# One long run of projections per unit on TensorE, and turns of B in the gate banks

## The reference

```python
proj = einsum('bsd,ed->bse', layernorm(x), in_proj_w)      # gate 8192, x 8192, B 1024, C 1024, dt 128
hBC = silu(causal_conv4(x, B, C))                          # depthwise, 4 taps, plus bias
xch = hs * dt                                              # 128 heads of 64, 4 chunks of 128 tokens
Y_diag = einsum('bzlhn,bzshn,bhzls,bzshp->bzlhp', C, B, L, xch)   # inside a chunk
states = einsum('bzlhn,bhzl,bzlhp->bzhpn', B, decay_states, xch)  # per chunk, then carried on
Y_off = einsum('bzlhn,bzhpn,bhzl->bzlhp', C, prev_states, exp(A_cum))
y = (Y_diag + Y_off + hs * D) * silu(gate)
out = rmsnorm over each of 8 groups of 1024 (y) * norm_w @ out_proj_w.T
```

## Time and profile before

| | |
|---|---|
| median of 3 runs | 1702.21 us (1701.96 to 1703.28) |
| profiled execution | 1699.52 us, span 1697.8 us |
| TensorE busy | 1624.3 us, 96% |
| VectorE busy | 1361.0 us, 80% |
| ScalarE busy | 1140.6 us, 67% |
| GpSimd busy | 836.5 us, 49% |
| mean granted TensorE clock | 0.986 of full |

### The profile page before, as it was taken

How to read it: one execution, slowest core, us unless ns; L and a number is a source line. 1 busy time by engine, 2 the same in 40 slices (tenths; PEclk the granted TensorE clock), 3 DMA queues, 4 the chain that set the end, 5 groups by cost and what they waited for, 6 DMA issues and landing times.

```text
span 1697.8 us, 26883 instructions
## 1 busy us (share of the span) xinstructions
PE 1624.3 (96%) x9616; PEld 1348.5 (79%) x9616; DVE 1361.0 (80%) x1974; ACT 1140.6 (67%) x2002; POOL 836.5 (49%) x543
## 2 busy tenths in 40 slices
PE   7779999999999999999999999999999999999987
PEld 5668888888888888878888888888888788888876
DVE  6467787987789878897879878898788978798766
ACT  5477767776687667767677766866677676777721
POOL 1135544564455544465445644555444654456542
PEclk9789999999999999999999999999999999999989
DMA  5423232323323232322323232222323223232211
GB/s 199 174 91 110 81 107 86 108 71 116 96 86 100 91 104 87 110 93 80 108 85 109 70 115 97 91 94 95 102 84 110 95 80 107 87 107 80 84 41 50
DMA packets 88244, 164.56 MB, mean 97 GB/s; under 512 B 23344, under 2 KB 39728, under 8 KB 87856
## 3 DMA queue, kind: packets, MB, share of 16 engines
q1 hardware_dynamic: 88112, 162.85, 29.2%
HBM read 157.03 MB, written 5.77 MB: 96 GB/s over the span
## 4 chain that ended last, share of the span: by engine, by line
PE 65%; DVE 13%; issue 9%; POOL 6%; ACT 3%; DVEq 0%; POOLq 0%; ACTq 0%
PE g_bank L713 6%; PE g_bank L715 6%; PE g_bank L714 6%; PE x_bank L713 5%; PE x_bank L715 4%; PE x_bank L714 4%; PE state_bank L722 4%; PE d_bank L731 4%; DVE mixed L1173 4%; PE state_bank L738 4%; PE x_bank L772 3%; PE x_bank L770 3%; PE x_bank L771 3%; PE d_bank L772 3%; PE d_bank L770 3%
## 5 line engine op out<-in xcount | busy, mean ns | idle before, releaser
L1323 POOL TENSOR_TENSOR y<-y,gate 128x512 f32<-128x512 f32 x128 | 223.3, 1744 | 457.5 <-DVE y L1140 457.5
L930 ACT ACTIVATE scores<-scores,tables 128x128 f32<-128x128 f32 x1024 | 312.4, 390 | 1.7 <-DMA scores<-sums_dram 1.7
L1078 DVE SCALAR_TENSOR_TENSOR hs<-x_bank,cols,hs 128x1022 f32<-128x1022 f32 (+2 forms) x192 | 244.7, 1274 | 85.2 <-ACT hs L940 82.9
L713 PE MATMUL g_bank<-x_high,w_high 128*128 128x512 f32 x624 | 258.8, 415 | 0.7 <-DVE bc L1156 0.7
L1330 POOL TENSOR_TENSOR xdecay<-xdt,tables 128x384 f32<-128x384 f32 x128 | 144.2, 1127 | 227.6 <-DVE xdt L1150 227.6
L715 PE MATMUL g_bank<-x_high,w_low 128*128 128x512 f32 x624 | 246.5, 395 | 0.0
L714 PE MATMUL g_bank<-x_low,w_high 128*128 128x512 f32 x624 | 244.7, 392 | 0.0
L1309 POOL TENSOR_TENSOR w_low<-raw,w_high 128x512 fp32r<-128x512 f32 x141 | 192.6, 1375 | 92.6 <-ACT w_high L920 92.6
L713 PE MATMUL x_bank<-x_high,w_high 128*128 128x512 f32 x512 | 214.1, 418 | 0.5 <-PEq L146 0.5
L715 PE MATMUL x_bank<-x_high,w_low 128*128 128x512 f32 x512 | 202.3, 395 | 0.0
L714 PE MATMUL x_bank<-x_low,w_high 128*128 128x512 f32 x512 | 201.0, 393 | 0.0
(11 more groups left out here) (172 smaller groups left out, 3680.5 us busy)
## 6 DMA issues: line engine op xcount, KB each, us to landing
scores<-sums_dram SPq DMA_DIRECT2D x128, 512.0 KB, 5.0
raw<-w_in SPq DMA_DIRECT2D x144, 256.0 KB, 2.9
grown_rows<-grown_dram SPq DMA_DIRECT2D x256, 96.0 KB, 2.7
out_raw<-w_out SPq DMA_DIRECT2D x64, 256.0 KB, 3.1
xt<-x SPq DMA_DIRECT2D x8, 256.0 KB, 5.3
mixed<-x SPq DMA_DIRECT2D x1, 2048.0 KB, 11.9
out<-mixed SPq DMA_DIRECT2D x8, 256.0 KB, 2.0
table_dram<-table SPq DMA_DIRECT2D x2, 768.0 KB, 3.2
```

What stands on the lines that cost most here:

```text
L713: pe.matmul(to, w_high[:, slot, k], x_high[:, b, k], start=(k == 0), stop=False)
L930: op = s.activation(at, at, ACT.Relu, bias=col[:, r, c:c + 1], scale=-1.0)
L1078: v.scalar_tensor_tensor(out=hs[:, q % 2, :, i:], in0=x_bank[:, :, 0:SEQ - i], scalar=cols[:, q, TAPS - 1 - i:TAPS - i], in1=hs[:, q % 2, ...
L1323: pool.tensor_tensor(y[:, b], y[:, b], gate[:, q % 2, b], ALU.mult).then_inc(y_ready, 1)
```

## The change

TensorE's `body` gets a new order: x tiles of both batches and gate tiles of both batches follow each other as 48 matmuls, then states of batch 0, both diagonals, carry of batch 0, output tiles 0 and 1, the projection of B or C where there is one, states of batch 1, turns of B at the group's end, the turn of batch 0, output tile 2, carry of batch 1, output tile 3, the turn of batch 1. `turn_b` writes both batches to the gate banks in place of the turn bank, and `keep_b` copies both at once. On ScalarE `decays` is parted in `differences` and `decays`, with tap 0 between them for batch 1, and the splits of output weights and of the first weight tile stand ahead of `finish`. On VectorE the three taps stand together ahead of `carried_state` of batch 0, the second `score` follows it, and the additions of output tiles are spread between the carry steps.

```diff
--- before.py
+++ after.py
@@ -753,7 +753,7 @@
 
             def turn_b(b):
                 for c in range(LATER):
-                    mm = pe.transpose(turn_bank[:, c * P:(c + 1) * P], bc_conv[:, 0, b, c * P:(c + 1) * P], ident[:])
+                    mm = pe.transpose(g_bank[:, b, c * P:(c + 1) * P], bc_conv[:, 0, b, c * P:(c + 1) * P], ident[:])
                 mm.then_inc(b_turned, 1)
 
             def var_of():
@@ -810,47 +810,31 @@
                         bc_of(1)
                     if ahead:
                         pe.wait_ge(conv_ready, k + 1)
-                        reached(pe, added, emptied(k - 1, 0))
-                        project(ahead[0], x_at, 0, x_bank[:, 0])
+                        for b in range(BATCH):
+                            reached(pe, added, emptied(k - 1, b))
+                            project(ahead[0], x_at, b, x_bank[:, b])
+                        pe.wait_ge(gate_ready, BATCH * (k + 1))
+                        if j in (5, 6) and not last:
+                            pe.wait_ge(bc_conv_ready, 2 * (g + 1) + j - 4)
+                        if turn_over:
+                            pe.wait_ge(bc_ready, g + 2)
+                        if j == 0:
+                            pe.wait_ge(b_tok_ready, g + 1)
+                        for b in range(BATCH):
+                            project(ahead[0], x_at + 1, b, g_bank[:, b])
+                    if j in (0, UNITS) and flush:
+                        done = g + j // UNITS
+                        pe.wait_ge(square_added, (UNITS - 1) * done)
+                        pe.wait_ge(xdt_ready, BATCH * (k + 1) if now else BATCH * ALL)
+                        var_of()
                     if now:
-                        if j == 0:
-                            pe.wait_ge(b_tok_ready, BATCH * (g + 1))
                         states(k, 0)
-                    if turn_over:
-                        pe.wait_ge(xdt_ready, BATCH * (k + 1))
-                        turn_b(0)
-                    if ahead:
-                        reached(pe, added, emptied(k - 1, 1))
-                        project(ahead[0], x_at, 1, x_bank[:, 1])
-                    if now:
                         for b in range(BATCH):
                             reached(pe, added, emptied(k - 1, 2 + b))
                             diagonal(k, s, b)
                         if j == 0:
                             pe.wait_ge(c_ready, g + 1)
                         carry(k, 0)
-                    if j in (0, UNITS) and flush:
-                        done = g + j // UNITS
-                        pe.wait_ge(square_added, (UNITS - 1) * done)
-                        pe.wait_ge(xdt_ready, BATCH * (k + 1) if now else BATCH * ALL)
-                        var_of()
-                    if ahead:
-                        pe.wait_ge(gate_ready, BATCH * k + 1)
-                        if j in (5, 6) and not last:
-                            pe.wait_ge(bc_conv_ready, 2 * (g + 1) + j - 4)
-                        if turn_over:
-                            pe.wait_ge(bc_ready, g + 2)
-                        project(ahead[0], x_at + 1, 0, g_bank[:, 0])
-                    if now:
-                        states(k, 1)
-                    if turn_over:
-                        pe.wait_ge(b_tok_ready, BATCH * (g + 1) + 1)
-                        turn_b(1)
-                    if ahead:
-                        pe.wait_ge(gate_ready, BATCH * k + 2)
-                        project(ahead[0], x_at + 1, 1, g_bank[:, 1])
-                    if now:
-                        carry(k, 1)
                     if flush:
                         pe.wait_ge(y_low_ready, k - j % 2)
                         pe.wait_ge(out_low_ready, k - j % 2)
@@ -860,24 +844,33 @@
                             else:
                                 pe.wait_ge(added, emptied(k - 1, c))
                             out_product(j, c)
+                    if j in (4, 5) and not last:
+                        for b in range(BATCH):
+                            pe.wait_ge(gate_ready, BATCH * (k + 1) + b + 1)
+                            project(g, (NEXT_B, NEXT_C)[j - 4], b, g_bank[:, b])
+                    if now:
+                        states(k, 1)
+                    if turn_over:
+                        pe.wait_ge(gate_ready, BATCH * (k + 2))
+                        turn_b(0)
+                        turn_b(1)
                     if ahead:
-                        if turn_over:
-                            pe.wait_ge(b_tok_ready, BATCH * (g + 1) + 2)
-                        elif j == 0:
+                        if j == 0:
                             reached(pe, std_ready, g)
                         pe.wait_ge(xdt_ready, BATCH * (k + 1))
                         turn_hs(k + 1, (j + 1) % 2, 0)
-                    extra = {4: NEXT_B, 5: NEXT_C}.get(j) if not last else None
-                    for c in (2, 3):
-                        if extra is not None:
-                            pe.wait_ge(gate_ready, BATCH * (k + 1) + c - 1)
-                            project(g, extra, c - 2, g_bank[:, c - 2])
-                        if flush:
-                            if now:
-                                pe.wait_ge(skip_added, k + 1)
-                            else:
-                                pe.wait_ge(added, emptied(k - 1, c))
-                            out_product(j, c)
+                    if flush:
+                        if now:
+                            pe.wait_ge(skip_added, k + 1)
+                        else:
+                            pe.wait_ge(added, emptied(k - 1, 2))
+                        out_product(j, 2)
+                    if now:
+                        carry(k, 1)
+                    if flush:
+                        if not now:
+                            pe.wait_ge(added, emptied(k - 1, 3))
+                        out_product(j, 3)
                     if ahead:
                         pe.wait_ge(xdt_ready, BATCH * (k + 1) + 1)
                         turn_hs(k + 1, (j + 1) % 2, 1)
@@ -885,17 +878,15 @@
             pe.wait_ge(bc_conv_ready, 1)
             for b in range(BATCH):
                 project(0, 0, b, x_bank[:, b])
-            pe.wait_ge(bc_silu, 1)
-            turn_b(0)
             pe.wait_ge(bc_silu, 2)
             for b in range(BATCH):
                 bc_of(b)
-            pe.wait_ge(b_tok_ready, 1)
-            turn_b(1)
             pe.wait_ge(bc_ready, 1)
             for b in range(BATCH):
                 project(0, 1, b, g_bank[:, b])
-            pe.wait_ge(b_tok_ready, 2)
+            pe.wait_ge(gate_ready, BATCH)
+            turn_b(0)
+            turn_b(1)
             turn_hs(0, 0, 0)
             pe.wait_ge(xdt_ready, 1)
             turn_hs(0, 0, 1)
@@ -919,7 +910,7 @@
                 reached(s, projected, BATCH * (n + 1 - SPLIT))
                 s.activation(w_high[:, slot], raw[:, slot], ACT.Copy).then_inc(w_high_ready, 1)
 
-            def decays(k, g, q, b):
+            def differences(k, g, q, b):
                 if q % HALF == 0:
                     s.wait_ge(tables_in[b][q // HALF], 16 * (g + 1))
                 s.wait_ge(sums_in[q % 2][b], 16 * (HALF * g + q // 2 + 1))
@@ -929,6 +920,8 @@
                         at = scores[:, q % 2, b, r, c]
                         op = s.activation(at, at, ACT.Relu, bias=col[:, r, c:c + 1], scale=-1.0)
                 op.then_inc(relu_ready, 1)
+
+            def decays(k, q, b):
                 s.wait_ge(relu_ready, BATCH * k + b + 1)
                 s.activation(scores[:, q % 2, b], scores[:, q % 2, b], ACT.Exp, scale=-1.0).then_inc(exp_ready, 1)
 
@@ -959,10 +952,10 @@
                 s.wait_ge(projected, BATCH * tile_number(g, place(g, q) + 1) + b + 1)
                 s.activation(gate[:, q % 2, b], g_bank[:, b], ACT.Silu).then_inc(gate_ready, 1)
 
-            def keep_b(g, b):
-                s.wait_ge(b_turned, BATCH * g + b + 1)
-                reached(s, states_added, BATCH * (UNITS * g - 1) + b + 1)
-                s.activation(b_tok[:, b].rearrange("p c n -> p (c n)"), turn_bank[:, 0:LATER * P], ACT.Copy)\
+            def keep_b(g):
+                s.wait_ge(b_turned, BATCH * (g + 1))
+                reached(s, states_added, BATCH * UNITS * g)
+                s.activation(b_tok[:].rearrange("p b c n -> p b (c n)"), g_bank[:, :, 0:LATER * P], ACT.Copy)\
                  .then_inc(b_tok_ready, 1)
 
             def keep_c(g):
@@ -1000,19 +993,18 @@
                         keep_c(g)
                     if j in (5, 6) and not last:
                         bc_tap0(g, j - 5)
-                    if prev:
-                        finish(*prev)
-                    if j == UNITS - 1 and not last:
-                        keep_b(g + 1, 0)
                     if now:
                         s.wait_ge(out_raw_in[j % 2], 16 * (HALF * g + j // 2 + 1))
                         reached(s, out_done, CHUNKS * (k - 2))
```

(57 more changed lines are left out.)

## The result

The changed kernel takes 1717.26 us (median of 4 runs, 1716.36 to 1717.65) against 1702.53 us (1701.96 to 1703.28) before: ratio 1.0085, 95% interval [1.0068, 1.0103]. It is slower, by 14.7 us. Forecast were 1711 and a range of 1687 to 1733.

The account below looks back on a forecast made before the run. TensorE, busy 1624.3 of 1697.8 us, was taken as the bound. Terms -7.4 - 10.6 + 11.3 + 13.0 + 2 + 0.5 = +8.8 on 1699.5 gave 1708.3, plus 2.7 to the median: 1711 us, range 1687 to 1733.

Parts of the forecast that it names:

- gaps, 62 units: TensorE: two fewer breaks and merged wide runs shorten each unit by 0.12 us; -7.4 us over 62 units.
- waits at the group change, 7: TensorE around the change of group: all 1.52 us of waits go, 7 times; -10.6 us.
- units 2 and 3, new wait less old, 14: TensorE at carry(k, 0): waits 2.4 us for carried_state, against 1.59 lost now; +0.8 x 14 = +11.3 us.
- units 5 and 6, new wait, 14: TensorE at carry(k, 0), B or C taps delaying VectorE: a new 0.93 us wait, 14 times; +13.0 us.
- rival (c): TensorE's clock falls in the new waits, 2 to 4 us each: 1732 or 1753; chance 0.14 together with (d).
- start and end: First exponentials delayed by B's copy, +0.5 us; last unit's state and final addition to y later, +2 us.
- (b): Whole kernel: gaps and group changes give 18 us, new waits take about that; 1702 us; chance 0.14.
- (a): VectorE keeps up, carried_state(k, 0) ending at 13.6; units 5 and 6 don't wait; -15.5, 1687 us; chance 0.27.
- (d): The scores' load is the bound: 2 us slower gives some 1 us every unit, +60; chance 0.14 with rival (c).

Follow-up runs that it names:

- squares_late: Changed kernel, GpSimd adding the squares behind its two weight splits, not ahead of out_low, in units 2, 3, 5 and 6: 1661.47 us.
- one_break_more: The changed kernel with late squares on GpSimd (1661.47 us), plus states(k, 0) moved back between x tiles and gate tiles: 1663.10 us.
- before_keep_b_later: Kernel before, add_squares behind the splits in units 2 and 3 (1675.83 us), plus ScalarE's group-change copy of B put behind tap 0: 1668.76 us.
- filler: Changed kernel with 8 more wide matmuls, read by nobody, ahead of carry(k, 0) in units 2 and 3 of groups 1 to 7: 1704.81 us.

## Why the prediction was right, and where it was off

By its own terms, against the two profiled executions:

| term | forecast, us | measured, us |
|---|---|---|
| gaps, 62 units | -7.4 (0.12) | -11.8 (0.19) |
| waits at the group change, 7 | -10.6 | -10.3 (2.04 less 3 x 0.19 each) |
| units 2 and 3, new wait less old, 14 | +11.3 (2.4) | +10.1 (2.31) |
| units 5 and 6, new wait, 14 | +13.0 (0.93) | +13.6 (0.97) |
| falls of the clock | 0, rival (c) at 2 to 4 each | +14.3 (9 x 1.59) |
| start and end | +2.5 | +2.2 (the rest) |
| sum | +8.8 | +18.1 |

**The mechanism was right in place and size.** Laid out from rows of before, with taking turns between VectorE and GpSimd, the state in unit 2 was to end at 16.0 and the carry to start at 16.05; it started 15.95 after the first x matmul. In units 5 and 6 the same held: the score was to be over at 7.25, y_low at 9.5 and the state at 14.5, and in unit 5 (first x matmul at 597.65) they were over at 7.3, 9.5 and 14.6. squares_late shows the cause: it leaves TensorE's and VectorE's order and work as they are and moves one instruction on GpSimd, and the waits go. So it is the order of GpSimd's queue, and not VectorE's load or the late diagonal as such. The Trainium skill's rule (SBUF, Who interferes with whom: issue order, not the shape of an operation, decides who blocks) is what the 4.86 us for three instructions of 8 columns bear out.

**Gaps were mis-sized.** The forecast counted breaks: by one_break_more one costs 0.06 in a long run, so two make its 0.12. Counted from start to start in an ordinary unit, what pays is how many wide matmuls stand far back in a run. In the third to twelfth place they follow each other at 0.231 us before; beyond the twelfth, where 36 stand after and none before, at 0.227. That is about 0.15 of the 0.19. The earlier trace rows already had these prices, 2.84 us for a first dozen against 2.72 for a dozen deep in a run. The waits of the group change went, but before_keep_b_later shows that they were not bound to the run of 48 or to VectorE's taps: one line on ScalarE removes the larger of them.

**The clock was a rival and became part of the outcome.** The sum put the falls at nothing; (c) named them, for the waits of 2.4 us. With nine of them the forecast would have been 1711 + 9 x 1.59 = 1725, by its price of 3 a fall 1738. That price came from reading the clock line's 0.8 as exact: the slice's granted clock was 0.88, so it lost 5.1 us and not 8.5.

That the forecast without the falls came out only 6 us low is luck in part. The gaps gave 4.4 more than forecast. And 2.7 us were added to come from the profiled execution to the median, where the profiled execution of the changed kernel stands 0.4 above its median: from profile to profile the miss is 9.3. The kernel that the forecast described, with the waits and without the falls, is filler, with 1704.81 us: 6 us under the forecast, just under its own range, and nearer to (b)'s 1702. So the waits were forecast rightly, one by one, and most of the 14.7 us by which the kernel became slower are the falls. Whether a wait of 2.2 us ends in a fall isn't settled by its length alone: five of fourteen equal ones kept 2.4 GHz, four of them in groups 1 and 2. What decides it among them no run shows.

**Rivals (a), (b) and (d)** fell. (a) needed the state by 13.6, and it came at 15.9. For (d), ScalarE does wait for the sums, but VectorE takes the exponentials later than they end: TensorE's steady waits are all at the carry, and squares_late has none with the same loads.

**The start** holds a wait that the forecast does not name: 7.71 us at the first carry. It cost little, as it came in the place of others: up to unit 2 TensorE waits 12.0 us from the first diagonal on, and 10.8 before.

## What to carry to other kernels

When two engines exclude each other, as VectorE and GpSimd do here in operations on two SBUF tensors, count turns, not work. A chain of n short instructions on one can pay n whole instructions of the other, and moving one long instruction in the *other* engine's queue won more here than the reordering of the busiest engine. Before reordering a saturated TensorE, lay out from measured durations when each product's last operand comes in the new order; the shorter gaps here were worth 0.7%, the operands that came late twice that. A wait in which TensorE idles 2.2 us in place of 1.4 may cost more than its length, as the clock can fall behind it; matmuls that nobody reads, put into that wait, bought it back. And before crediting a new order with a wait that went, look for the one instruction that it hung on: nearly all the waits that the kernel before had in its steady part went without the new order.

## What the runs showed of the hardware

- A VectorE operation of 8 columns on two SBUF tensors still waits for GpSimd's whole instruction: 4.86 us for three in a row, against 6.29 for three of 512 columns.
- After equal waits of 2.2 us the clock fell to 1.2 GHz for 3.4 us in nine cases of fourteen; each cost 1.59 us. Eight matmuls in the wait kept it at 2.4 GHz in all fourteen. Waits of 1.4 us never brought it down in the steady part of the kernel before, nor did those of 0.8 and 0.9 us in the others.
- A break of six narrow matmuls in a run of wide ones costs 0.06 us beyond their own time, though the dozen behind it runs at 0.237 us each rather than 0.227: the first of them starts 0.08 early.
